# Cross-attention and decoder layer on one Trainium2 core: a new order of work in the first two groups of the first phase

## The chip, the cores and the metric

The kernel runs on one core of a Trainium2 chip. The metric is the device time of one launch in microseconds (us), the median of several runs. The core has TensorE (PE, matmuls), VectorE (DVE), ScalarE (ACT), GpSimd (POOL) and SyncE (SP), which issues most of the DMAs. Each engine runs its own program in order and waits on semaphores.

## The reference

Two layers over `x` (32 batches, 112 tokens, 512 wide). The first, which is all that this change touches, attends to a memory of 375 rows of 256:

```python
memory_proj = einsum('bme,de->bmd', memory, W_mem)
scores = einsum('bnd,bmd->bnm', x, memory_proj) / sqrt(512)
attn = softmax(scores)
memory_context = einsum('bnm,bmd->bnd', attn, memory_proj)
gate = sigmoid(einsum('bnf,df->bnd', concat([x, memory_context]), W_gate) + b_gate)
x = rmsnorm(x + gate * memory_context, norm_w)
```

The second is a decoder layer with two experts. `expert_mask` looks at the mask of the tokens (both a token and its successor padded), and each token goes through the one or the other set of weights (`v_*`, `l_*`): rotary self-attention, cross-attention to the memory, a gated MLP. Its order of tokens is by expert, so the kernel needs, before the first token is written, each token's rank among those of its expert.

## The kernel before, in words

Every fp32 operand is split into a high part (a copy rounded to the matmul's type, fp32r) and a low part (source minus high part), and each product is three matmuls: high by high (L111), high by low (L112), low by high (L113), in `split_products`. ScalarE makes most high parts, VectorE or GpSimd the low parts (`low`, L179). Weights come through a ring of 8 slots: SP loads (L188), ScalarE copies (`ring_high`, L201), GpSimd subtracts (`ring_low`, L179). Chunks 0 and 1 are for `u`, 2 and 3 for `context` (C_MC), 4 to 7 for `gate` (C_GATE).

The first phase takes the 32 batches in 8 groups of 4 (`NB`), and its order is written out by hand in one function for each engine: `a_sp`, `a_pool`, `a_act`, `a_pe`, `a_dve`. For a group g TensorE runs, in this order:

- `u(g)`: x times the combined weights, in two halves t of 128 rows; split by `u_high` (ACT L550) and `u_low` (DVE L752);
- `s0(g)`: the scores, u against the memory's transpose `m_hi`, `m_lo`, also in two halves t, with the four batches inside a half. The memory comes in two halves too: load (SP L471 or L485), `memory_high` (ACT L545), `memory_low` (DVE L179 with 1500 columns). The load of a half waits for the `memory_low` of the half before, since both use one buffer;
- softmax on DVE (L759, L763, L765) and ACT (L564);
- `gate(g-1)`: the gate of the group before, 72 matmuls; ACT applies tanh (L577), DVE forms the fused value in `gated` (L783, L786). The last of these releases the load of x for group g+1 (L474). Inside the fourth part are the transposes of the first two batches (L680, `transposed`);
- `attended(g, b)`: probabilities times memory (L688) for each batch, once DVE has copied the transposed probabilities (L797); then ACT copies the result (L589) and DVE subtracts (`attended_low`, L179 with 224 columns);
- `turn(g-1)`: transposes of the fused values (L698), squares on ACT (L603), power on POOL (L517), tokens on DVE (L823), and a scatter of the rows by POOL (L525);
- `context(g)`: 24 matmuls (L111 to L113).

Into group 0 and group 1 the one-time work is woven. `setup_pe_wc` multiplies W_mem and the memory's part of the gate weights (24 matmuls of 512 columns); `setup_dve_weights`, `setup_act_wc` and `setup_dve_wc` split its inputs and results. The ranks: `setup_dve` compares the mask (L330 to L332) and prepares the rotary positions (L334 to L339); `setup_pe` sums over the batches (L299, L300); `setup_dve_total` copies the totals (L343); `setup_pe_ranks` (L304, L306, L308) ranks them; `setup_dve_ranks` and `setup_dve_counts` (L348 to L381) count; `setup_pe_places` (L312) and `setup_dve_places` (L385 to L403) follow; `setup_dve_slots` (L410 to L433) makes the slots, and with them (L429) POOL starts six scatters of padding (L269 to L271), for which the squares of group 0 and `names(0)` (L814) wait.

## Time and profile before

| | |
|---|---|
| median of 3 runs | 2202.34 us (2202.33 to 2205.23) |
| the profiled execution's own time | 2200.88 us |
| its span | 2199.0 us |
| PE busy | 2103.6 us, 96% of the span |
| DVE, ACT, POOL busy | 1279.3, 1048.8, 879.2 us |
| granted TensorE clock, mean | 0.986 |
| first phase (groups 0 to 7) | about the first 340 us of the span |

A timeline row gives the start in us from the span's start, the duration in us (for a group, from its first start to its last end), the engine, the line, the operation, output and input, the count, and in brackets how long the engine had been idle and what released it. Matmuls overlap, so the distance between two starts, not the duration, is what one costs.

### The profile page before, as it was taken

What the parts mean: (1) busy time and instruction counts of PE and PEld (TensorE: products, weight loads), DVE (VectorE), ACT (ScalarE), POOL (GpSimd) and SP (SyncE); (2) the same over time, 40 slices, a digit from 0 to 9 for tenths busy, and PEclk for the clock granted to TensorE, in tenths of its full rate; (3) what the DMA queues carried; (4) which work ended last, traced back from release to release, by engine and by line L of the source; (5) the groups of instructions that cost most, each with busy time, mean ns of one, the idle gap of its engine ahead of it and who ended that gap; (6) DMA issues with size and microseconds to landing.
All of it is one profiled execution on the core that took longest, in us unless ns stands there. A gap on an engine that the chain in (4) does not pass through costs nothing.

```text
span 2199.0 us, 40731 instructions
## 1 busy us (share of the span) xinstructions
PE 2103.6 (96%) x16042; PEld 1821.3 (83%) x16042; DVE 1279.3 (58%) x2070; ACT 1048.8 (48%) x1875; POOL 879.2 (40%) x741
## 2 busy tenths in 40 slices
PE   7999999999888889997999999999999999999998
PEld 6899998888767777996899899877888888888888
DVE  6755547666589994445676676663444344443433
ACT  5344445343268774542665655654334333343334
POOL 2211026776635333633112112114455554555547
PEclk9999999999999999997999999999999999999999
DMA  6334344655564446656777777745343443434334
GB/s 241 123 131 147 115 158 151 238 204 212 200 202 141 138 136 239 242 199 197 229 231 228 218 216 222 213 138 194 115 138 119 134 151 114 139 117 125 119 94 130
DMA packets 155614, 373.70 MB, mean 170 GB/s; under 512 B 40160, under 2 KB 60992, under 8 KB 145696
## 3 DMA queue, kind: packets, MB, share of 16 engines
q1 hardware_dynamic: 136416, 310.70, 45.0%
q0 software_dynamic: 18720, 60.29, 7.5%
q8 instruction: 128, 2.10, 0.4%
q14 instruction: 62, 0.51, 0.1%
q10 hardware_dynamic: 288, 0.11, 0.0%
HBM read 269.28 MB, written 100.93 MB: 168 GB/s over the span
## 4 chain that ended last, share of the span: by engine, by line
PE 82%; DVE 9%; DMA 3%; ACT 3%; issue 2%; SPq 1%; POOLq 0%; POOL 0%; ACTq 0%; DVEq 0%
PE ps L111 21%; PE ps L113 21%; PE ps L112 21%; PE ps L1853 4%; PE ps L1885 3%; PE ps L1872 3%; DVE f_arena L1311 2%; DVE c_max L1306 2%; PE ps L688 2%; ACT f_arena L1767 1%; DMA f_arena<-qk_rows 1%; DVE c_sum L1317 1%; PE ps L1900 1%; PE ps L2201 1%; DVE f_arena L1328 1%
## 5 line engine op out<-in xcount | busy, mean ns | idle before, releaser
L111 PE MATMUL ps<-r_arena 128*128 128x512 f32 (+6 forms) x2410 | 893.1, 371 | 13.5 <-DVE r_arena L179 7.2
L113 PE MATMUL ps<-r_arena 128*128 128x512 f32 (+6 forms) x2410 | 882.5, 366 | 0.0
L112 PE MATMUL ps<-r_arena 128*128 128x512 f32 (+6 forms) x2410 | 882.2, 366 | 0.0
L179 POOL TENSOR_TENSOR r_arena<-f_arena,r_arena 128x512 fp32r<-128x512 f32 (+1 forms) x434 | 579.3, 1358 | 542.3 <-ACT r_arena L201 418.7
L111 PEld LDWEIGHTS ps<-r_arena 128*128 128x128 f32 (+2 forms) x2410 | 455.6, 189 | 77.1 <-POOL r_arena L179 6.2
L113 PEld LDWEIGHTS ps<-r_arena 128*128 128x128 f32 (+2 forms) x2410 | 454.5, 189 | 65.7
L112 PEld LDWEIGHTS ps<-r_arena 128*128 128x128 f32 (+2 forms) x2410 | 455.6, 189 | 60.3
L201 ACT CAST r_arena<-f_arena 128x512 fp32r<-128x512 f32 x400 | 236.3, 623 | 173.0 <-PE ps L113 133.3
L1979 DVE TENSOR_REDUCE e_negmax<-ps 112x2 f32<-112x750 f32 (+1 forms) x352 | 240.4, 720 | 95.4 <-PE ps L1853 94.2
L2289 DVE SCALAR_TENSOR_TENSOR f_arena<-f_arena,ps 128x512 f32<-128x512 f32 (+1 forms) x88 | 57.4, 652 | 235.1 <-ACT f_arena L2184 230.7
L1767 ACT ACTIVATE f_arena<-ps 125x896 f32<-125x896 f32 x192 | 166.4, 924 | 46.3 <-PE ps L1872 46.3
L2188 ACT CAST r_arena<-ps 128x512 fp32r<-128x512 f32 (+1 forms) x88 | 49.3, 561 | 243.4 <-DVE ps L2293 243.4
L179 DVE TENSOR_TENSOR r_arena<-ps,r_arena 128x512 fp32r<-128x512 f32 (+2 forms) x186 | 102.6, 562 | 89.5 <-ACT r_arena L2188 55.1
L1730 POOL DMA_INDIRECT cd_rows<-f_arena,slot_all x32 | 30.0, 937 | 289.4 <-ACT f_arena L1810 289.4
L1853 PE MATMUL ps<-r_arena 96*112 96x376 f32 x512 | 129.9, 354 | 10.7 <-DVE e_negmax L1979 4.5
L2293 DVE SCALAR_TENSOR_TENSOR ps<-f_arena,ps 128x512 f32<-128x512 f32 (+1 forms) x88 | 58.3, 663 | 107.1 <-PE ps L113 106.9
L2184 ACT ACTIVATE f_arena<-ps 128x512 f32<-128x512 f32 (+1 forms) x88 | 50.2, 571 | 138.2 <-PE ps L113 138.2
L1872 PE MATMUL ps<-r_arena 98*125 98x224 f32 x768 | 109.0, 278 | 2.6 <-DMA r_arena<-r_arena 0.3
L1872 PEld LDWEIGHTS ps<-r_arena 98*125 98x125 f32 x768 | 100.0, 190 | 12.3 <-ACT f_arena L1767 8.5
L1853 PEld LDWEIGHTS ps<-r_arena 96*112 96x112 f32 x512 | 82.3, 182 | 23.3 <-DVE e_negmax L1979 11.2
L517 POOL TENSOR_TENSOR a_rstd<-a_ss,minus_half 112x2 f32<-112x2 f32 x16 | 11.3, 705 | 202.5 <-DVE a_ss L807 202.4
L1171 POOL TENSOR_TENSOR f_arena<-f_arena 112x448 f32<-112x448 f32 x32 | 36.4, 1139 | 135.2 <-ACT f_arena L1211 135.2
(213 smaller groups left out, 2566.6 us busy)
## 6 DMA issues: line engine op xcount, KB each, us to landing
f_arena<-weights SPq DMA_DIRECT2D x400, 256.0 KB, 3.0
r_arena<-k_rows SPq DMA_DIRECT2D x192, 188.0 KB, 3.6
k_rows<-r_arena SPq DMA_DIRECT2D x64, 376.0 KB
f_arena<-rows SPq DMA_DIRECT2D x14, 1160.0 KB, 5.2
f_arena<-qk_rows SPq DMA_DIRECT2D x32, 448.0 KB
f_arena<-mem_n SPq DMA_DIRECT2D x8, 1536.0 KB, 6.9
f_arena<-mem_e SPq DMA_DIRECT2D x32, 376.0 KB, 4.9
f_arena<-mem_t SPq DMA_DIRECT2D x16, 750.0 KB, 6.0
```

Of the source, the lines that this page charges most:

```text
L111: first = pe.matmul(out, w_hi, x_hi, start=start, stop=False)
L112: pe.matmul(out, w_hi, x_lo, start=False, stop=False)
L113: return first, pe.matmul(out, w_lo, x_hi, start=False, stop=stop)
L179: return engine.tensor_tensor(out, source, high.bitcast(F32), ALU.subtract)
L201: act.copy(w_hi[:, m % RING, :], w_raw[:, m % RING, :]).then_inc(w_hi_made, 1)
L1767: act.activation(e_pt[:, u], ps[0:KC, at:at + 2, 0:4 * SEQ], ACT.Exp).then_inc(e_exp, 1)
L1853: last = pe.matmul(ps[0:SEQ, at + h - heads[0], 0:CEVEN], e_queries[b % 3][0:MAX_ROW, h % 2, h // 2, :], e_keys[b % 3][0:MAX_ROW, h // 2, ...
L1872: last = pe.matmul(ps[0:KC, 4 + 2 * (u % 2) + n // 2, n % 2 * 2 * SEQ:(n % 2 + 1) * 2 * SEQ], e_keys[b % 3][0:MAX_ROW + 2, pair, m], e_que ...
L1885: last = pe.matmul(ps[32 * a:32 * a + 32, 3, batch(n)], e_cv[b % 4][:, c, 4 * n + a, :], e_pt[:, NKC * t + c, half, batch(a)], start=c == ...
L1979: dve.tensor_reduce(e_negmax[:, b % 2, heads[0]:heads[-1] + 1], ps[0:SEQ, at:at + len(heads), 0:CTX], AX_X, ALU.max, negate=True).then_inc ...
L2289: dve.scalar_tensor_tensor(act_a[:, s, w], act_t[:, s, w], 1.0, ps[:, bank, w], ALU.add, ALU.mult).then_inc(f_acted, 1)
L2293: dve.scalar_tensor_tensor(ps[:, bank + 1, w], act_a[:, s, w], 0.5, ps[:, bank + 1, w], ALU.mult, ALU.mult).then_inc(f_glu_made, 1)
```

## The change

It moves instructions inside the first phase and changes one wait; no operation is added or taken out. `u_high`, `u_low` and the memory's splits of group 0 alternate by half; `s0` waits for each half of the memory by itself; the splits of the gate weights move ahead of group 0's attended copies on ACT; the mask part of `setup_dve` becomes `setup_dve_valid` ahead of the combined weights' splits on DVE, and the second of these splits moves behind two copies; `setup_pe` moves ahead of `context(0)` on PE; `setup_dve_total` moves ahead of the rest of `setup_dve`; `setup_dve_ranks` and `setup_dve_counts` move ahead of the first `u_low(1)`, and `memory_low(1, 1)` behind it; and for later groups the second `memory_low` moves out of the end of `gated` and behind the fourth copy of probabilities.

```diff
+        def setup_dve_valid(dve):
+            dve.wait_ge(const_loaded, 16 * len(loads))
+            dve.tensor_scalar(is_pad_s, mask_sb, 1, None, ALU.is_equal).then_inc(*d_steps.up())
+            dve.memset(ones_sb, 1.0).then_inc(*d_steps.up())
+            dve.wait_ge(*d_steps.now())
+            dve.tensor_tensor(is_v_s, is_pad_s[:, 0], is_pad_s[:, 1], ALU.mult).then_inc(s_isv, 1)
...
-            dve.wait_ge(const_loaded, 16 * len(loads))
-            now(dve.tensor_scalar(is_pad_s, mask_sb, 1, None, ALU.is_equal))
-            now(dve.memset(ones_sb, 1.0))
-            dve.tensor_tensor(is_v_s, is_pad_s[:, 0], is_pad_s[:, 1], ALU.mult).then_inc(s_isv, 1)
...
             for t in range(CT):
                 memory_high(0, t)
-            u_high(0)
+                u_high(0, t)
...
                     setup_act_wc(act)
-                    for m in range(C_MC, C_GATE):
+                    for m in range(C_MC, RING):
                         ring_high(act, m)
...
                     setup_act_consts(act)
-                    for m in range(C_GATE, RING):
-                        ring_high(act, m)
...
             def s0(g):
-                pe.wait_ge(a_m_lo, CT * (g + 1))
                 if g:
                     pe.wait_ge(a_mc_made, KT * g)
                 for t in range(CT):
+                    pe.wait_ge(a_m_lo, CT * g + t + 1)
                     pe.wait_ge(a_u_lo, CT * g + t + 1)
...
+                if g == 0:
+                    setup_pe(pe)
                 if g < GROUPS:
                     context(g)
-                if g == 0:
-                    setup_pe(pe)
...
-                if g + 2 < GROUPS:
-                    memory_low(g + 2, 1)
...
             for t in range(CT):
                 memory_low(0, t)
-            for t in range(CT):
                 u_low(0, t)
             setup_dve_weights(dve)
             softmax(0)
-            setup_dve_wc(dve)
+            setup_dve_valid(dve)
+            setup_dve_wc(dve, 0)
...
                     attended(0, 0)
                     attended(0, 1)
+                    setup_dve_wc(dve, 1)
                 if g < GROUPS:
                     for b in range(NB):
                         if b + 2 < NB:
                             attended(g, b + 2)
+                        if b == 1 and g and g + 1 < GROUPS:
+                            memory_low(g + 1, 1)
                         attended_low(g, b)
...
                 else:
+                    setup_dve_total(dve)
                     setup_dve(dve)
                     memory_low(1, 0)
                     x_low(1)
-                    setup_dve_total(dve)
-                    memory_low(1, 1)
+                    setup_dve_ranks(dve)
+                    setup_dve_counts(dve)
                 if g + 1 < GROUPS:
                     for t in range(CT):
                         u_low(g + 1, t)
                         if g == 0 and t == 0:
-                            setup_dve_ranks(dve)
-                            setup_dve_counts(dve)
+                            memory_low(1, 1)
```

How the order moves is seen at three places. The first is VectorE between group 0's attended copies and group 1's scores; before it reads (L343 is the copy of the totals, the 128x448 rows are x's low parts, the 128x1500 rows the memory's):

```order
L338 TENSOR_SCALAR f_arena<-f_arena 112x112
L339 TENSOR_TENSOR f_arena<-f_arena 112x112
L179 TENSOR_TENSOR r_arena<-f_arena,r_arena 128x1500
L179 TENSOR_TENSOR r_arena<-f_arena,r_arena 128x448 x4
L343 COPY f_arena<-ps 32x128
L179 TENSOR_TENSOR r_arena<-f_arena,r_arena 128x1500
L752 SCALAR_TENSOR_TENSOR r_arena<-ps,r_arena 128x448
```

and now (lines have shifted by a few numbers; L346 is the copy of the totals):

```order
L346 COPY f_arena<-ps 32x128
L337 CAST f_arena<-f_arena 112x112
L338 CAST f_arena<-f_arena 112x112
L339 TENSOR_SCALAR f_arena<-f_arena 112x112
L340 TENSOR_TENSOR f_arena<-f_arena 112x112
L341 TENSOR_SCALAR f_arena<-f_arena 112x112
L342 TENSOR_TENSOR f_arena<-f_arena 112x112
L179 TENSOR_TENSOR r_arena<-f_arena,r_arena 128x1500
L179 TENSOR_TENSOR r_arena<-f_arena,r_arena 128x448 x4
L351 COPY f_arena<-ps 112x32
```

The totals are copied before the six position steps and both sorts of low parts, and the ranks (L351) follow x's low parts at once.

The second place is ScalarE between the combined weights' splits and group 1's x. Before:

```order
L294 CAST r_arena<-ps 128x512 x2
L201 CAST r_arena<-f_arena 128x512 x2
L589 CAST r_arena<-ps 128x2x112 x4
L545 CAST r_arena<-f_arena 128x1500
L280 CAST causal<-f_arena 112x448
L281 CAST ident_b<-ident 128x128
L282 ACTIVATE half_b<-gate_b 128x4
L201 CAST r_arena<-f_arena 128x512 x4
L537 CAST r_arena<-f_arena 128x448 x4
```

and now:

```order
L294 CAST r_arena<-ps 128x512 x2
L201 CAST r_arena<-f_arena 128x512 x6
L589 CAST r_arena<-ps 128x2x112 x4
L547 CAST r_arena<-f_arena 128x1500
L280 CAST causal<-f_arena 112x448
L281 CAST ident_b<-ident 128x128
L282 ACTIVATE half_b<-gate_b 128x4
L539 CAST r_arena<-f_arena 128x448 x4
```

The four gate weights' copies (part of L201) now stand ahead of the four attended copies (L589).

The third is VectorE in group 1, as in groups 2 to 6: the end of `gated` and the attended copies. Before:

```order
L783 SCALAR_TENSOR_TENSOR f_arena<-f_arena 128x448
L786 SCALAR_TENSOR_TENSOR f_arena<-f_arena 128x448
L179 TENSOR_TENSOR r_arena<-f_arena,r_arena 128x1500
L797 COPY f_arena<-ps 125x336
L179 TENSOR_TENSOR r_arena<-ps,r_arena 128x2x112
L797 COPY f_arena<-ps 125x336
L179 TENSOR_TENSOR r_arena<-ps,r_arena 128x2x112 x3
```

and now:

```order
L782 SCALAR_TENSOR_TENSOR f_arena<-f_arena 128x448
L785 SCALAR_TENSOR_TENSOR f_arena<-f_arena 128x448
L794 COPY f_arena<-ps 125x336
L179 TENSOR_TENSOR r_arena<-ps,r_arena 128x2x112
L794 COPY f_arena<-ps 125x336
L179 TENSOR_TENSOR r_arena<-f_arena,r_arena 128x1500
L179 TENSOR_TENSOR r_arena<-ps,r_arena 128x2x112 x3
```

The 128x1500 row, the memory's low part, now follows both copies, with three of the four attended low parts behind it.

## Rows read from the trace of the kernel before

**Rows 1.** Waits of PE, 100 to 300 us: total us, times, longest us.

```profile
PE ps L688 <- DVE f_arena L797: 4.5, 5, 0.9
```

**Rows 2.** Timeline of PE, first 100 us: start, duration, and idle time before.

```profile
15.95 0.40 PE L111 MATMUL ps<-r_arena 128*112 128x376 f32 x1 [2.89 <-DVE r_arena L752]
...
21.67 0.40 PE L111 MATMUL ps<-r_arena 128*128 128x512 f32 x1
...
36.32 0.47 PE L111 MATMUL ps<-r_arena 128*128 128x448 f32 x1 [0.86 <-DVE r_arena L179]
...
46.71 0.58 PE L304 MATMUL ps<-f_arena 32*112 32x32 f32 x2 [4.61 <-DVE f_arena L343]
...
47.99 0.72 PE L111 MATMUL ps<-r_arena 128*128 128x448 f32 x1
...
55.60 0.39 PE L312 MATMUL ps<-f_arena 112*128 112x14 f32 x2 [1.06 <-DVE f_arena L381]
...
75.94 1.56 PE L688 MATMUL ps<-f_arena 125*128 125x112 f32 x12 [0.51 <-DVE f_arena L797]
...
81.48 4.56 PE L688 MATMUL ps<-f_arena 125*128 125x112 f32 x24 [1.98 <-DVE f_arena L797]
```

**Rows 3.** Busy time by stretch; the number after POOL is the granted clock.

```profile
18.00:20.00 2.00, 2.00 (x8) 1.94 (x8) 2.00 (x5) 1.00 (x2) 0.00 (x0) 0.50 0.99 350
...
36.30:41.40 5.10, 5.08 (x25) 4.46 (x25) 4.12 (x11) 5.07 (x11) 2.72 (x2) 1.00 0.11 14
...
46.70:55.80 9.10, 8.03 (x32) 7.06 (x32) 4.54 (x11) 1.09 (x2) 0.49 (x2) 0.76 0.30 106
...
79.30:86.00 6.70, 4.72 (x28) 4.54 (x28) 3.53 (x6) 0.79 (x3) 0.00 (x0) 0.75 0.52 176
```

**Rows 4.** Timeline of DVE, first 100 us.

```profile
16.95 3.63 DVE L179 TENSOR_TENSOR r_arena<-f_arena,r_arena 128x1024 fp32r<-128x1024 f32 x5 [0.61 <-ACT r_arena L287]
...
36.18 0.18 DVE L330 TENSOR_SCALAR f_arena<-f_arena 112x64 f32<-112x64 int32 x1
...
38.27 1.72 DVE L179 TENSOR_TENSOR r_arena<-f_arena,r_arena 128x1500 fp32r<-128x1500 f32 x1
40.67 5.78 DVE L179 TENSOR_TENSOR r_arena<-f_arena,r_arena 128x448 fp32r<-128x448 f32 x4 [0.68 <-ACT r_arena L537]
...
69.32 0.17 DVE L429 TENSOR_SCALAR f_arena<-f_arena 128x2 int32<-128x2 f32 x1
...
75.29 0.91 DVE L797 COPY f_arena<-ps 125x336 f32<-125x336 f32 x2
...
88.33 2.23 DVE L179 TENSOR_TENSOR r_arena<-f_arena,r_arena 128x448 fp32r<-128x448 f32 x4 [0.28 <-ACT r_arena L537]
...
91.02 2.72 DVE L823 SCALAR_TENSOR_TENSOR f_arena<-ps,a_rstd,norm 112x512 f32<-112x512 f32 x4
```

**Rows 5.** Timelines of ACT and of POOL, first 100 us.

```profile
86.58 0.60 ACT L603 ACTIVATE f_arena<-ps 112x512 f32<-112x512 f32 x1 [0.15 <-PE ps L698]
...
38.68 7.29 POOL L179 TENSOR_TENSOR r_arena<-f_arena,r_arena 128x512 fp32r<-128x512 f32 x4 [7.66 <-ACT r_arena L201]
```

**Rows 6.** Loads: first and last issue, time to landing (memory half; last two gate weights).

```profile
L471 SPq DMA_DIRECT2D f_arena<-mem_t x1: 439/439/439, 17.9 to 17.9; - x1
...
DMA to landing us min/median/max: 8.0/8.0/8.0
...
L188 SPq DMA_DIRECT2D f_arena<-weights x2: 450/468/485, 19.8 to 20.3; - x2
...
DMA to landing us min/median/max: 10.3/10.3/10.4
```

**Rows 7.** The chain that ended last: load and copy of memory (2, 1).

```profile
73.02 4.77 DMA f_arena<-mem_t
77.81 1.45 ACT r_arena L545
```

**Rows 8.** The last padding scatter, L271, issued at 77.1 us: time to landing.

```profile
DMA to landing us min/median/max: 7.1/7.1/7.1
```

More of the change, by code:

```diff
@@ L357, in setup_dve_weights, with setup_dve_wc @@
                 low(dve, wg_lo[:, k, :], wg_raw[:, k, :], wg_hi[:, k, :]).then_inc(s_lo, 1)
-        def setup_dve_wc(dve):
-            for t in range(CT):
-                dve.wait_ge(wc_hi_made, t + 1)
-                low(dve, wc_lo[:, t, :], ps[:, 6 + t, :], wc_hi[:, t, :]).then_inc(wc_lo_made, 1)
+        def setup_dve_wc(dve, t):
+            dve.wait_ge(wc_hi_made, t + 1)
+            low(dve, wc_lo[:, t, :], ps[:, 6 + t, :], wc_hi[:, t, :]).then_inc(wc_lo_made, 1)
         WHOLE = TILES - 1
@@ L545, in memory_high, with u_high @@
                 act.copy(m_hi[:, t, 0:NB * CTX], memt if g else memt_first[t]).then_inc(a_m_hi, 1)
-            def u_high(g):
-                for t in range(CT):
-                    act.wait_ge(a_u, CT * g + t + 1)
-                    act.activation(l_hi[:, t, :], ps[:, 6 + t, 0:NT], ACT.Copy,
-                                   scale=float(DIM) ** -0.5).then_inc(a_u_hi, 1)
+            def u_high(g, t):
+                act.wait_ge(a_u, CT * g + t + 1)
+                act.activation(l_hi[:, t, :], ps[:, 6 + t, 0:NT], ACT.Copy, scale=float(DIM) ** -0.5).then_inc(a_u_hi, 1)
             ring_high(act, 0)
@@ L617, in a_act @@
                 if g + 1 < GROUPS:
-                    u_high(g + 1)
+                    for t in range(CT):
+                        u_high(g + 1, t)
         def a_pe(pe):
@@ L832, in a_dve @@
                 memory_low(0, t)
-            for t in range(CT):
                 u_low(0, t)
```

## The prediction

> **What bounds the kernel now.** I read four views in this order. The page gives TensorE 2103.6 us of a span of 2199.0 (96%): it is the engine to save time on, in waits or in matmuls that run slowly. The waits of PE show where it idles in the first phase: from 100 to 300 us one wait alone, 0.9 us in each of five groups, for VectorE's copy L797 [rows 1]. The timeline of PE shows the others, all in the first 82 us: 2.89 us before the first scores, 0.86 before `context(0)`, 4.61 before the ranks (L304), 1.06 before L312, then 0.51 and 1.98 before L688 [rows 2]. The stretches show what a wait also costs: the granted clock was 0.50 (the lower level, 1.2 GHz) at 18 to 20 us, and averaged 0.76 at 46.7 to 55.8 and 0.75 at 79.3 to 86, each time after a wait of PE, and 1.00 at 36.3 to 41.4 [rows 3]. After the waits of 0.86 and 0.9 us the rows show no such loss. The timelines of the other engines say what is late in each place.
>
> The first phase hands a chain of work to the next without any fixed time in it, so what PE gains by the end of group 6 I carry to the end of the kernel.
>
> **Scores and weights of group 0.** The first scores wait for `u_low(0,0)`, which stood behind both memory halves. By halves, one memory low part (1.72 us [rows 4]) no longer stands in front: they start near 14.1 instead of 15.95 [rows 2], and end 1.9 us (clock as before) to 3.3 us earlier. Little of it arrives: the next matmuls (`setup_pe_wc`, at 21.67 [rows 2]) need the gate inputs' low parts, which VectorE finishes at 16.95 + 3.63 = 20.58 whatever the scores do [rows 4]. Gain 1.1 at most; a new wait of some 2 us stands in front, and if the clock falls there it takes up to 1.6 back (eight matmuls of 512 columns at half speed).
>
> **Group 0's attended part.** VectorE now makes one split less before its first copy, but ScalarE becomes the late one: four more copies stand ahead of its first L589, and the last of these needs a load issued at 20.3 that landed 10.4 us later, at 30.7 [rows 6]. With a copy of some 0.55 ScalarE is free at 31.25 and starts its first L589 there. From there: L589 0.35, low part 0.38, copy of the fourth batch 0.45 (two in 0.91 [rows 4]) to 32.4, its matmuls 1.4 (12 in 1.56, overlap included [rows 2]), L589 and low part 0.75: `context(0)` starts at 34.5 to 35.2 instead of 36.32 [rows 2]. I take 34.8, **1.5 us**. The two matmuls of `setup_pe` fall into the wait of 0.86 there. The mask work now stands in front of the first copy and waits for nine constant loads. No row shows their landing. The load behind them on the same queue, issued at 17.9, landed 8.0 later, at 25.9 [rows 6], and VectorE comes for them at about 25.2. So I take a wait of 0 to 0.7, hidden by ScalarE until 31.25. The farthest bound is their first use before, L330 at 36.2 [rows 4]: a rival.
>
> **From `context(0)` to group 1's scores.** 24 matmuls at 0.204 (25 in 5.1 us [rows 3]) end at 39.7. The wait of 4.61 goes: the totals are copied at 34.9. Then VectorE has six position steps (1.6 us of the 2.1 from L330 to the next memory half, 36.18 to 38.27 [rows 4]), `memory_low(1,0)` 1.7 and x's low parts. These took 5.78 us while GpSimd made the four gate weights' low parts (7.29 us); in group 1 the same four took 2.23 [rows 4, 5]. GpSimd now has its work at 30 to 35, beside copies and subtractions out of PSUM, and I take 2.23: x is ready at 40.4. The Trainium skill (GPSIMD Engine Reference, Specifications) says that GpSimd shares its SBUF interfaces with VectorE where a VectorE instruction has two SBUF inputs; the rows agree, and by that rule the gate weights' low parts would not be slowed where they now stand. The ranks' six matmuls took 1.28 (46.71 to 47.99 [rows 2]), less at the full clock: `u(1)` starts at 40.8, **5.7 more** (7.2 in all). Were x's low parts still 5.78 us, 3.5 of this chain would be lost.
>
> `u(1)` ran from 47.99 to 54.54 (55.60 less the wait of 1.06 [rows 2]), 6.55 us, in part at the lower clock; with PE busy right up to it I take 24 x 0.204 = 4.9: **1.6**. The wait of 1.06 before L312 goes too, since the counts are done at about 43.5: **1.06**. `s0(1)` starts at 46.0, 9.8 us early. Its second half needs `memory_low(1,1)`: load issued 38.2, landed 4 us later, ScalarE to 43.7, VectorE to 46.5, then `u_low(1,1)` 47.1; that half starts at 48.1. Covered with 1 us to spare.
>
> **Group 1.** VectorE is late here, not PE. Its places (L385) started as L312 ended, at 55.60 + 0.39 [rows 2]; now they start at 47.1, 8.9 early, and everything behind them (softmax, slots, `gated(0)`) is the same work: the copies for `attended(1)` come at 66.4 instead of 75.29, and PE, ready at 65.5, waits 1.5 instead of 0.51. 0.9 of the 9.8 is lost. Then the third copy no longer stands behind `memory_low(2,1)`, which stood behind a load of 4.77 us and a ScalarE copy of 1.45 [rows 7]. The wait of 1.98 [rows 2] with 0.2 of issue goes: **2.2**. The 24 matmuls behind it took 4.56 us where 12 such took 1.56, overlap included [rows 2]: at 1.4 for twelve, **1.8** if the clock holds. The load still stands ahead of ScalarE's L589: landed 68.9, copied 70.35, L589 70.7, fourth copy 71.55, needed 71.75. So it fits barely. `turn(0)` ends at 74.9, 12.9 early.
>
> What is late next is the padding. The last scatter, issued at 77.1, landed 7.1 later at 84.2 [rows 8], 14.7 us behind the slots (L429 ends at 69.49 [rows 4]). Now the slots come at 60.6, so it lands at 75.3, and the squares, which started at 86.58 behind PE's first turn [rows 5], could start at 73.55 and wait. `u(2)` needs the second token: 91.02 + 1.36 = 92.4, or 5.8 behind the first square. That gives 81.15 against an end of `context(1)` at 79.75: **-1.4**.
>
> **Groups 2 to 6.** The 0.9 us wait was for a copy behind `memory_low` (1.72). Now the copy goes first, as soon as PE's transposes are there. The low part then ends some 1 us before `turn` does, so `context` does not wait: 5 x 0.9 = **4.5** [rows 1]. Group 7 had no such low part.
>
> **Sum.** 1.5 + 5.7 + 1.6 + 1.06 - 0.9 + 2.2 + 1.8 - 1.4 + 4.5 = 16.0 us. The profiled execution's own time was 2200.88, so 2184.9 by it; the median of the runs is 1.46 higher, and I predict **2186.3**.
>
> The clock is the weakest term. The Trainium skill (TensorE: Matmul & The Clock Gate, What's actually happening) says that the watching runs free, so that one kernel shows different numbers of slow matmuls. By that rule the stretches of rows 3 could fall elsewhere in the new program, after its waits near 18.4, 65.5 and 79.8. From the rows each is worth up to 1.8 us.
>
> **Rivals.**
>
> (a) *A slow stretch returns in group 1* after the wait of 1.5 us, or `memory_low(2,1)` and the fourth copy miss by a little and PE stops again. Against: no loss after 0.9. For: a loss after 1.98. Gain 16.0 - 1.8 - 1.0 = 13.2: 2189.1. Chance 0.15.
>
> (b) *Groups 2 to 6 give nothing*: `memory_low` now stands ahead of three low parts that `context` needs. If it were slowed by more than the 1 us of slack, the wait moves from the copy to `context`. Gain 11.5: 2190.8. Chance 0.05.
>
> (c) *The change doesn't start where it says*: the constants land late, and VectorE holds the mask work in front of its first copy. PE's first attended matmuls then follow that landing. At the farthest bound, 36.2, the copy comes some 7.5 us later than I take and 8.5 are left: 2193.8. Chance 0.05.
>
> (d) *More*: slow stretches stay away at 18 us too and the scatters, with less beside them, land in time: + 0.5 + 1.4: 2184.4. Chance 0.13.
>
> (e) *Slower*: the clock falls at the wait before `u(2)` (79.8 to 81.2) and stays at the lower level. Matmuls then cost twice, so it outweighs the gain once 16 us of full-speed work have run so; a whole group (38 us) gives 2186.3 + 38 = 2224. Against: every stretch of the trace came back within 7 us, and groups 2 to 6 with waits of 0.9 never fell. Chance 0.02. The same page (Seeing it yourself) tells of records stuck at a low ratio for over 50 us; no row here shows that.
>
> **How the numbers follow.** Forecast 0.60. The range 2183.0 to 2190.6 takes in (d), the forecast with 2 us either way of clock and run, and (a); it leaves out (b), (c), (e). A measurement of this kernel can tell about 0.2% (4.4 us) from no change. Faster by more than that: all but (e) and worse mixtures of (b) and (c): 0.95; within it 0.03; slower 0.02.
>
> **What would show it.** L304 and L312 without a wait before them; `u(1)` near 41 us and 4.9 us long; `s0(1)` at 46; x's low parts in about 2.2 us; the wait before L304 replaced by none longer than 2.3 us anywhere; the attended matmuls of group 1 in one clock; ScalarE's squares of group 0 waiting for the last scatter; no wait for the copy from 100 to 300 us, and none for L179 or L589 in its place. A first L589 after 33 us, x's low parts over 4 us, or a granted clock of 0.5 after 55 us would make me wrong.

## The result and the profile after

| | before | changed |
|---|---|---|
| median, runs taken side by side | 2202.34 us (5 runs, 2198.42 to 2205.23) | 2190.04 us (5 runs, 2186.0 to 2190.69) |
| the profiled execution's own time | 2200.88 us | 2186.00 us |
| its span | 2199.0 us | 2184.1 us |
| PE busy | 2103.6 us | 2096.5 us |

The ratio is 0.9937, with an interval of 0.9925 to 0.9948: 13.9 us less, and between 11.5 and 16.5 us by the interval. The prediction said faster, 2186.3 us, within 2183.0 to 2190.6. The direction is right and the range holds the median, near its upper end. The working is best judged inside the trace, where each term has a place.

The timeline of PE of the changed kernel, rows at the places of [rows 2], and the last row at the end of the first phase:

```profile
14.05 0.33 PE L111 MATMUL ps<-r_arena 128*112 128x376 f32 x1
...
20.55 0.47 PE L111 MATMUL ps<-r_arena 128*128 128x512 f32 x1 [2.20 <-DVE r_arena L179]
...
34.74 0.47 PE L111 MATMUL ps<-r_arena 128*128 128x448 f32 x1 [0.21 <-DVE r_arena L179]
...
39.80 0.38 PE L304 MATMUL ps<-f_arena 32*112 32x32 f32 x2
...
40.53 0.45 PE L111 MATMUL ps<-r_arena 128*128 128x448 f32 x1
...
45.84 0.40 PE L111 MATMUL ps<-r_arena 128*112 128x376 f32 x1
...
67.75 1.56 PE L687 MATMUL ps<-f_arena 125*128 125x112 f32 x12 [2.21 <-DVE f_arena L794]
...
71.14 2.84 PE L687 MATMUL ps<-f_arena 125*128 125x112 f32 x24
...
73.82 1.91 PE L697 MATMUL ps<-ident,f_arena 128*112 128x128 f32 x16
...
82.38 0.47 PE L111 MATMUL ps<-r_arena 128*128 128x448 f32 x1 [1.78 <-DVE f_arena L820]
...
319.41 1.91 PE L1013 MATMUL ps<-ident,f_arena 128*128 128x128 f32 x16
```

The ranks (L304) have no wait in front, `u(1)` starts at 40.53, `s0(1)` at 45.84. The 24 matmuls of the third and fourth batch take 2.84 us, where [rows 2] had 4.56. Three waits of about 2 us are left: before the product of the weights (20.55), before `attended(1)` (67.75) and before `u(2)` (82.38). In the profile of before the last row stood at 335.79, so the first phase ends 16.4 us sooner.

The waits of PE of the changed kernel, 0 to 100 us, in the columns of [rows 1]; from 100 to 300 us this view has no row any more, where [rows 1] had 4.5 us in five waits:

```profile
PE ps L111 <- DVE r_arena L179: 8.4, 3, 6.0
PE ps L687 <- DVE f_arena L794: 2.6, 2, 2.2
PE ps L111 <- DVE f_arena L820: 1.8, 1, 1.8
```

The timeline of VectorE of the changed kernel, with the answers to [rows 4]:

```profile
24.90 0.19 DVE L326 TENSOR_SCALAR f_arena<-f_arena 112x64 f32<-112x64 int32 x1
...
34.60 0.27 DVE L346 COPY f_arena<-ps 32x128 f32<-32x128 f32 x1
34.80 1.19 DVE L337 CAST f_arena<-f_arena 112x112 f32<-112x112 int32 x1
...
37.30 3.86 DVE L179 TENSOR_TENSOR r_arena<-f_arena,r_arena 128x1500 fp32r<-128x1500 f32 x5
...
47.77 0.22 DVE L387 TENSOR_SCALAR f_arena<-f_arena 128x7 f32<-128x7 f32 x1
...
61.13 0.17 DVE L431 TENSOR_SCALAR f_arena<-f_arena 128x2 int32<-128x2 f32 x1
...
67.10 0.92 DVE L794 COPY f_arena<-ps 125x336 f32<-125x336 f32 x2
...
76.47 0.29 DVE L811 COPY f_arena<-cos_sin 112x256 f32<-112x256 f32 x1 [1.68 <-DMA cd_rows<-f_arena,pad_slot]
```

The mask work (L326) runs at 24.90 without a wait, so the constants were there. The memory's low part and x's four together take 3.86 us, against 1.72 and 5.78 in [rows 4]. The row of L337 is the one I had not foreseen: an int32 to fp32 cast of 112x112 takes 1.19 us. The same cast took 0.21 us before.

The timeline of GpSimd of the changed kernel, at that cast:

```profile
27.49 7.42 POOL L179 TENSOR_TENSOR r_arena<-f_arena,r_arena 128x512 fp32r<-128x512 f32 x6 [17.14 <-ACT r_arena L201]
34.85 1.07 POOL L263 MEMSET f_arena<- 128x1160 f32 x1
```

The memset ends at 35.92 and the cast at 35.99. ScalarE of the changed kernel has the other two places, its first attended copy and the first square of group 0:

```profile
31.06 0.58 ACT L589 CAST r_arena<-ps 128x224 fp32r<-128x224 f32 x2
...
76.47 0.60 ACT L601 ACTIVATE f_arena<-ps 112x512 f32<-112x512 f32 x1 [2.10 <-DMA cd_rows<-f_arena,pad_slot]
```

### The profile page after: what moved, and what is told of

Same layout as the page of the kernel before. It is cut to its first block, busy times and chain, and to the rows that moved or that the text cites. A ratio compares the mean times of both kernels' runs of the same rounds, so it can differ in the third digit from the quotient of the medians.

```text
span 2184.1 us, 40739 instructions
## 1 busy us (share of the span) xinstructions
PE 2096.5 (96%) x16042; PEld 1815.5 (83%) x16042; DVE 1276.0 (58%) x2070; ACT 1049.1 (48%) x1875; POOL 876.5 (40%) x741
## 4 chain that ended last, share of the span: by engine, by line
PE 80%; DVE 8%; DMA 5%; ACT 3%; SPq 2%; issue 2%; POOL 0%; POOLq 0%; ACTq 0%; DVEq 0%
PE ps L111 20%; PE ps L113 20%; PE ps L112 20%; PE ps L1853 4%; PE ps L1885 3%; PE ps L1872 3%; DMA f_arena<-qk_rows 2%; DVE f_arena L1311 2%; DVE c_max L1306 2%; PE ps L687 2%; ACT f_arena L1767 1%; DMA f_arena<-weights 1%; PE ps L1230 1%; PE ps L1900 1%; PE ps L2201 1%
## 5 line engine op out<-in xcount | busy, mean ns | idle before, releaser
L111 PE MATMUL ps<-r_arena 128*128 128x512 f32 (+6 forms) x2410 | 890.3, 369 | 13.9 <-DVE r_arena L179 8.6
L201 ACT CAST r_arena<-f_arena 128x512 fp32r<-128x512 f32 x400 | 236.5, 623 | 175.4 <-PE ps L113 129.6
```

Of the source, the lines that this page charges most:

```text
L111: first = pe.matmul(out, w_hi, x_hi, start=start, stop=False)
L201: act.copy(w_hi[:, m % RING, :], w_raw[:, m % RING, :]).then_inc(w_hi_made, 1)
```

## The experiments

Each variant starts from the changed kernel, except where it says from the kernel before. Medians are compared with the kernel before on the same chip: 2200.94 us for the first four, 2204.43 for the next four, 2201.35 for the last two. Beside the median stands the landmark that proved sharper: the first row of L1013, the end of the first phase, 335.79 before and 319.41 after. Each of these times comes from one profiled execution. A variant counts by its number here: variant 3 is the kernel of experiment 3.

**1. The memory's low part moved, and nothing else** (from the kernel before).

```diff
-                if g + 2 < GROUPS:
-                    memory_low(g + 2, 1)
...
+                        if b == 1 and g and g + 1 < GROUPS:
+                            memory_low(g + 1, 1)
                         attended_low(g, b)
```

> The kernel before with one part of the change alone: the second memory low part of groups 2 to 7 behind the copies. My theory: the waits before L688 in groups 2 to 6 go, each worth 1.16 us from start to start (the idle column shows 0.9 because a matmul's modelled end overlaps), so 5.8 us; in group 1 the wait of 1.98 and the slow stretch behind it go too, but then the squares wait for the last padding scatter, which leaves 2 to 2.5 there. Sum about 8 us faster, near 2194. Rival (the low part becomes late for context): a wait of PE for L179 before context in groups 2 to 6, and under 3 us gained.

Measured: 2193.76 us, ratio 0.9963 (0.9949 to 0.9976); the phase ends at 326.76, 9.0 us sooner. Of the 9.0 us, 2.8 are there when `u(2)` starts (89.75 instead of 92.50) and 6.3 come in groups 2 to 6. No wait is left from 100 to 300 us, and the third batch of group 1 starts without one and at the full clock:

```profile
79.16 2.84 PE L688 MATMUL ps<-f_arena 125*128 125x112 f32 x24
...
326.76 1.91 PE L1013 MATMUL ps<-ident,f_arena 128*128 128x128 f32 x16
```

**2. The same move taken back, and all else kept.**

```diff
+                if g + 2 < GROUPS:
+                    memory_low(g + 2, 1)
...
-                        if b == 1 and g and g + 1 < GROUPS:
-                            memory_low(g + 1, 1)
                         attended_low(g, b)
```

> The changed kernel with that same part undone. If the parts add up, it loses 5.8 us in groups 2 to 6 against the changed kernel and up to 2 us in group 1, where the wait for the load of the memory's second half comes back: 6 to 8 us slower than the changed kernel, so about 7 us faster than before, near 2196. If the gain of the set-up parts were given back later, it would stand within 3 us of before.

Measured: 2197.05 us, ratio 0.9976 (0.9966 to 0.9986). Its timeline and waits of PE:

```profile
74.89 4.56 PE L687 MATMUL ps<-f_arena 125*128 125x112 f32 x24 [1.80 <-DVE f_arena L796]
...
329.29 1.91 PE L1013 MATMUL ps<-ident,f_arena 128*128 128x128 f32 x16
```

```profile
PE ps L687 <- DVE f_arena L796: 4.5, 5, 0.9
```

The five waits of 0.9 are back, and so is the wait in group 1 (1.80) with its 24 slow matmuls: 4.56 us, the very number of [rows 2]. The first two groups' new order is worth 6.5 us by itself, the low part's move 9.0. They add up to 15.5, against 15.8 for the repeat of the changed kernel below, which has the same slow product of the weights as variant 2. At the landmark the two parts add up within 0.3 us.

**3. GpSimd's two memsets at the start of its program**, away from VectorE's position steps.

```diff
+            pool.memset(tok[:, 0:PADS, :], 0.0).then_inc(pads_zeroed, 1)
+            pool.wait_ge(pads_zeroed, 1)
+            pool.memset(tok[:, PADS:NB, DIM:ROW], 0.0).then_inc(pads_zeroed, 1)
             for m in range(RING):
                 ring_low(pool, m)
-            pool.memset(tok[:, 0:PADS, :], 0.0).then_inc(pads_zeroed, 1)
-            pool.wait_ge(pads_zeroed, 1)
-            pool.memset(tok[:, PADS:NB, DIM:ROW], 0.0).then_inc(pads_zeroed, 1)
```

> The changed kernel with GpSimd's two memsets for the padding moved to the program's start, where it idles. Theory: the integer cast L337, 1.19 us in the changed kernel beside the memset and 0.21 before, is slowed by that memset; it goes back to about 0.2, VectorE's places, slots and first copies of group 1 come 1.0 us sooner, and PE's wait before the first attended matmuls of group 1 falls from 2.2 to about 1.2. About 1 us faster than the changed kernel. Rival (the cast is slow for another reason, such as ScalarE's copies beside it): the cast stays at 1.2 and nothing moves.

Measured: 2187.4 us, ratio 0.9934 (0.992 to 0.9947); the phase ends at 319.38. VectorE and GpSimd of this variant:

```profile
35.88 0.57 DVE L337 CAST f_arena<-f_arena 112x112 f32<-112x112 int32 x1
```

```profile
28.93 7.45 POOL L179 TENSOR_TENSOR r_arena<-f_arena,r_arena 128x512 fp32r<-128x512 f32 x6 [18.83 <-ACT r_arena L201]
```

The cast is shorter, not yet 0.2. GpSimd's last low part ends at 28.93 + 7.45 = 36.38, the cast at 36.45. What holds the cast is thus whatever GpSimd has running, not the memset as such. The 1 us that was expected is not there at the landmark: the phase ends 0.03 us sooner than in the first profile of the changed kernel and 0.6 sooner than in its repeat. PE still waits 2.00 us before `attended(1)`, and this profile has a slow stretch there.

**4. Group 0's squares written elsewhere** (with edit 3). Only their sum is used; as their own output they now take the buffer of the probabilities, in bf16, instead of the token rows, so that ScalarE need not wait for the padding scatters.

```diff
+        p0_half = fv(12252, (NB * CTX,), SEQ).bitcast(BF16)
...
-                    else:
-                        act.wait_ge(pads_scattered, 16 * 3 * PADS)
+                    aside = g == 1
...
-                        act.activation(tok[0:SEQ, b, 0:DIM], ps[0:SEQ, turn_bank(b), :], ACT.Square,
+                        act.activation(p0_half[:, b * DIM:b * DIM + DIM] if aside else tok[0:SEQ, b, 0:DIM], ps[0:SEQ, turn_bank(b), :], ACT.Square,
```

> The kernel of the run memset_early, and the squares of group 0 write their unused result (in bf16) to the probabilities' buffer, so they need not wait for the padding scatters; only the names on VectorE still do. Theory: the wait of 2.10 us of ScalarE for the last scatter and the wait of 1.78 of PE before u(2) go or shrink to under 0.5: 1.5 to 2 us faster than memset_early, some 2.5 to 3 faster than the changed kernel. Rival: VectorE's names wait for the scatter as long, with x's low parts behind them, and PE's wait stays above 1.2.

Measured: 2184.81 us, ratio 0.9918 (0.9903 to 0.9932), the lowest ratio of all, though the first phase shows only a small part of that gain; the phase ends at 318.93, 0.45 before variant 3. ScalarE of this variant:

```profile
74.98 0.60 ACT L601 ACTIVATE f_arena<-ps 112x512 bf16<-112x512 f32 x1
...
77.39 1.97 ACT L540 CAST r_arena<-f_arena 128x448 fp32r<-128x448 f32 x4 [1.14 <-DMA f_arena<-x_t]
```

The squares no longer wait, but two of them later ScalarE waits 1.14 us for group 2's x, and PE still 1.02 before `u(2)` (1.78 in the changed kernel's first profile, 1.06 in its repeat, both with the scatters). So the scatters do hold the squares of the changed kernel, and right behind them stands the load of x: x's high parts start at 77.39, against 77.63 in that first profile. The 1.5 to 2 us that were expected over variant 3 are not there for that reason.

**5. The wait before the product of the weights filled** with ten matmuls whose result nobody reads. This and variant 9 add work that is no part of the computation.

```diff
             s0(0)
+            for _ in range(10):
+                pe.matmul(ps[:, 4, 0:NT], x_parts[0][0][:, 0, 0:P], x_parts[0][0][:, 0, :], start=True, stop=True)
             setup_pe_wc(pe)
```

> The changed kernel with ten matmuls of 448 columns, whose result nobody reads, in the wait of 2.2 us between the first scores and the weights' product. In the changed kernel's profile the granted clock stayed at 1.00 there; in three profiles of its variants it read 0.76 from 20 to 27 us and the product's 24 matmuls took 7.15 us instead of 5.56. Theory: the fall comes from the wait and varies from run to run; filled, the clock reads 1.00 from 13 to 27 us in any run, the product ends by 26.3, context(0) starts by 34.9, and the median falls by 0.5 to 1.5 us against the changed kernel (2190.0). Rival (the fall has nothing to do with the wait): 0.76 again.

Measured: 2187.98 us, ratio 0.9924 (0.9905 to 0.9943); the phase ends at 319.80. The product ran at the full clock and `context(0)` started at 35.10. `context(0)` is thus 0.36 us later than in the first profile, which had the full clock there too, and 0.8 sooner than in the repeat. In this profile the clock fell one wait later, before `attended(1)`, as it did in variants 3, 7 and 8, which have no unread matmuls. This variant's timeline of PE:

```profile
20.89 0.47 PE L111 MATMUL ps<-r_arena 128*128 128x512 f32 x1 [0.20 <-DVE r_arena L179]
...
68.10 2.20 PE L687 MATMUL ps<-f_arena 125*128 125x112 f32 x12 [2.19 <-DVE f_arena L796]
...
73.12 2.84 PE L687 MATMUL ps<-f_arena 125*128 125x112 f32 x24
```

Twelve matmuls took 2.20 us behind a wait of 2.19; in the changed kernel they took 1.56 behind one of 2.21. From these twelve to the start of `turn(0)` it is 7.70 us here and 6.07 there, so the same wait can cost 1.6 us more or nothing. Little of it reaches the end: `u(2)` starts at 82.81 instead of 82.38, as the wait for the padding shrinks from 1.78 to 0.23.

**6. The copy of the totals back behind x's low parts.**

```diff
-                    setup_dve_total(dve)
                     setup_dve(dve)
                     memory_low(1, 0)
                     x_low(1)
+                    setup_dve_total(dve)
```

> The changed kernel with the copy of the totals back behind the position steps, the memory half and x's low parts. Theory: the wait of 4.61 before was mostly x's low parts slowed by GpSimd's gate splits; with those already done, x's low parts still end near 41.2, the copy at 41.4, and PE waits 1.7 us before L304: group 1 starts 1.5 to 2 us later, 1 to 2 us slower in all. Rival (the place of the copy itself made the wait): 4 us or more before L304 and 4 us slower.

Measured: 2188.36 us, ratio 0.9936 (0.9918 to 0.9953); the phase ends at 323.64. VectorE, GpSimd and PE of this variant:

```profile
35.89 1.75 DVE L337 CAST f_arena<-f_arena 112x112 f32<-112x112 int32 x1
```

```profile
36.49 1.08 POOL L263 MEMSET f_arena<- 128x1160 f32 x1
```

```profile
43.05 0.38 PE L304 MATMUL ps<-f_arena 32*112 32x32 f32 x2 [1.89 <-DVE f_arena L346]
```

The wait before L304 comes back, 1.89 us of it. Against the repeat, which has the same slow product, the places, which lead to the slots, start at 50.12 instead of 49.28, the last scatter lands 1.8 us later (7.4 us after its issue instead of 6.4), and `u(2)` starts at 85.04 instead of 83.16. At the landmark the difference is 3.7 us, and only 1.9 of it is there when `u(2)` starts. The rest comes inside group 2, mostly from the clock, which fell behind PE's wait of 2.11 us before `u(2)`. The stretch from 85 to 90 us of this variant (the number after POOL is the granted clock, 1.00 in the repeat):

```profile
85.00:90.00 5.00, 4.96 (x17) 4.47 (x18) 1.90 (x3) 0.69 (x2) 3.41 (x4) 0.66 0.54 167
```

So the later copy itself costs between 0.8 us, its delay of the slots, and 1.9; the other 1.8 need not come in each execution. The median does not show either: it is lower than that of the changed kernel.

**7. The copies of the gate weights back behind the constants** on ScalarE.

```diff
-                    for m in range(C_MC, RING):
+                    for m in range(C_MC, C_GATE):
                         ring_high(act, m)
...
                     setup_act_consts(act)
+                    for m in range(C_GATE, RING):
+                        ring_high(act, m)
```

> The changed kernel with ScalarE's four gate weight copies back behind the constants. Theory: ScalarE's first L589 no longer waits for the last load (31.06 us) and context(0) starts 0.5 to 1 us sooner, but the copies then delay x's high parts by 2.2 us and GpSimd's four low parts run beside x's low parts, which take over 5 us instead of 2.2: PE waits inside or before u(1), and the copies for group 1's attended part come 2.5 to 4 us later. 2.5 to 4 us slower than the changed kernel. Rival (no contention, the slowness of x's low parts before was ScalarE's): x's low parts in under 3 us and within 1 us of the changed kernel.

Measured: 2190.68 us, ratio 0.9941 (0.9924 to 0.9959); the phase ends at 322.66, 2.7 us behind the repeat. VectorE and GpSimd of this variant:

```profile
35.77 0.20 DVE L337 CAST f_arena<-f_arena 112x112 f32<-112x112 int32 x1
...
40.06 5.49 DVE L179 TENSOR_TENSOR r_arena<-f_arena,r_arena 128x448 fp32r<-128x448 f32 x4 [1.08 <-ACT r_arena L539]
```

```profile
28.82 2.51 POOL L179 TENSOR_TENSOR r_arena<-f_arena,r_arena 128x512 fp32r<-128x512 f32 x2 [19.01 <-ACT r_arena L201]
38.08 6.99 POOL L179 TENSOR_TENSOR r_arena<-f_arena,r_arena 128x512 fp32r<-128x512 f32 x4 [6.75 <-ACT r_arena L201]
```

With GpSimd's subtractions beside them x's low parts take 5.49 us again, as in [rows 4], and two waits of 0.75 appear in `u(1)`. So this move pays by keeping two engines' two-input subtractions apart, as the prediction had it. And the cast, with GpSimd idle from 31.33 to 38.08, takes 0.20 us.

**8. The halves undone**: group 0's scores wait for both memory halves, as before. On ScalarE both copies of `u(0)` go behind both memory halves again, too.

```diff
                 memory_low(0, t)
+            for t in range(CT):
                 u_low(0, t)
...
+                if g == 0:
+                    pe.wait_ge(a_m_lo, CT)
                 for t in range(CT):
-                    pe.wait_ge(a_m_lo, CT * g + t + 1)
+                    if g:
+                        pe.wait_ge(a_m_lo, CT * g + t + 1)
```

> The changed kernel with group 0's scores waiting for both halves of the memory, as before. Theory: the first scores start near 15.9 instead of 14.05 and end near 20.5 to 21.7; the weights' product starts then instead of at 20.55, so at most 1.1 us go in front, and ScalarE's wait for the gate weights (free at 31.1) hides half of it: 0 to 1 us slower, which these runs can hardly tell. The wait of 2.9 us puts the slow stretch into the scores instead of the product. Rival (the earlier scores carry through to the end): 1.9 us or more slower.

Measured: 2186.57 us, ratio 0.9925 (0.9908 to 0.9943); the phase ends at 318.92. Timeline of PE of this variant:

```profile
15.90 0.40 PE L111 MATMUL ps<-r_arena 128*112 128x376 f32 x1 [2.34 <-DVE r_arena L755]
...
20.67 0.47 PE L111 MATMUL ps<-r_arena 128*128 128x512 f32 x1 [0.42 <-DVE r_arena L179]
...
35.19 0.47 PE L111 MATMUL ps<-r_arena 128*128 128x448 f32 x1 [0.21 <-DVE r_arena L179]
```

The scores start 1.85 us later, the product only 0.12 and `context(0)` 0.45, and at the landmark nothing is lost. The halves only move the wait from the scores to behind them, and no gain of theirs is seen at the end. The slow stretch that was expected in the scores, behind the wait of 2.34, did not come either: the granted clock is 1.00 from 15 to 20 us.

**9. Edits 3, 4 and 5 together, and nine matmuls in the wait before `attended(1)`.**

```diff
                     pe.wait_ge(a_mn_loaded, 16 * (g + 1))
+                    for _ in range(9 if g == 1 else 0):
+                        pe.matmul(ps[:, 0, 0:NT], x_parts[1][0][:, 0, 0:P], x_parts[1][0][:, 0, :], start=True, stop=True)
```

> The changed kernel with four more edits: the memsets at the start, the squares aside, ten unread matmuls in the wait before the weights' product, and nine in the wait before group 1's attended part. Theory: the two waits are where the clock falls in some runs and not in others, so with both filled the granted clock reads 1.00 from 6 to 95 us; GpSimd is done with the gate splits by 35, so the cast L337 takes 0.2; the first u_low(2) comes by 84.3 instead of 85.7. Phase one ends 1.5 to 2.5 us sooner than in the changed kernel's profile; the median lies 2 to 4 us under that of the changed kernel in the same rounds. Rival: the clock falls anyway, the unread matmuls only delay, and it stands within 1 us of the changed kernel.

Its result stands with that of the next.

**10. The changed kernel again**, unedited, on the same chip.

> The changed kernel itself once more, beside the run combined on one chip. Theory: its own runs again spread over some 4 to 6 us, and its profile may show a slow stretch of TensorE at 20 to 27 us or at 60 to 75 us that the first profile did not; where it does, phase one ends 1 to 2 us later than there. Rival: the same profile as the first, within 0.3 us in phase one.

Measured: 2190.31 us, ratio 0.9944 (0.9931 to 0.9958), for the combination; 2189.71 us, ratio 0.9942 (0.9929 to 0.9956), for the repeat. The phase ends at 317.62 and at 319.95. The combination has the granted clock at 1.00 throughout the first 95 us, and its cast takes 0.20 us, with no work of GpSimd beside it after 34.56. So the first phase ends 2.3 us sooner than in the repeat and 1.8 sooner than in the first profile, and nothing of it is seen in the median, which was expected 2 to 4 us lower.

The repeat shows the slow product again. Its stretch from 20 to 27 us, then that of the changed kernel's first profile (the number after POOL is the granted clock):

```profile
20.00:27.00 7.00, 6.34 (x22) 5.14 (x23) 5.59 (x17) 3.14 (x9) 0.00 (x0) 0.76 1.04 351
```

```profile
20.00:27.00 7.00, 6.37 (x30) 5.24 (x30) 5.77 (x18) 3.71 (x11) 0.00 (x0) 1.00 1.03 358
```

One program, one wait (2.18 and 2.20 us), and 0.76 or 1.00. `context(0)` starts at 35.93 in the repeat instead of 34.74, yet the phase ends only 0.5 us later: the last scatter was issued 1.5 us later but landed after 6.4 us instead of 7.5, and so `u(2)` starts only 0.8 later.

**Why medians don't separate these variants.** Behind the first phase all kernels do the same work. From the first row of L1013 to the end of the span it took 1863.2 us before, 1864.7 after, 1862.4 in the repeat, 1863.7 in the combination and 1870.7 in variant 5. The stretch from 340 to 2180 us, of the repeat and then of variant 5:

```profile
340.00:2180.00 1840.00, 1772.90 (x14161) 1515.09 (x14159) 1069.16 (x1629) 892.38 (x1532) 806.15 (x663) 0.99 0.55 174
```

```profile
340.00:2180.00 1840.00, 1775.76 (x14139) 1516.84 (x14138) 1067.69 (x1624) 891.36 (x1530) 804.06 (x661) 0.98 0.55 174
```

Variant 5 keeps PE busy 2.9 us longer in that stretch, with 22 matmuls fewer recorded and at a lower mean clock. A part that no edit touches thus varies by 8 us, more than edits 3 to 9 are worth. The matmuls of a group vary a little too, at a granted clock of 1.00: from the start of `context` to the transposes inside the next gate it is between 25.53 and 25.76 us, with one such block for each of groups 2 to 6. The five take 127.7 us in the repeat and 128.7 in the combination, which was 3.2 us ahead when `u(2)` started and 2.3 at the end. I judge edits 3 to 9 by the landmark and by their own rows alone.

## Why the prediction was right, and where not

The table follows the sum term by term. The measured column takes differences of start times in the two profiles, before minus after.

| step | predicted | measured |
|---|---|---|
| to `context(0)` | 1.5 | 1.6 |
| to `u(1)`: the wait of 4.61 | 5.7 | 5.9 |
| to `s0(1)`: full clock, and the wait at L312 | 1.6 + 1.06 | 2.5 |
| VectorE late in group 1 | -0.9 | -1.8 |
| to `turn(0)`: the wait of 1.98 and the slow stretch | 2.2 + 1.8 | 3.9 |
| to `u(2)`: padding | -1.4 | -1.9 |
| groups 2 to 6 | 4.5 | 6.3 |
| end of the first phase | 16.0 | 16.4 |

The sum lies closer to the trace than its terms do. Groups 2 to 6 gave 1.8 us more than forecast; the late VectorE and the padding took 1.4 more. That these nearly cancel is luck, and so is the full clock behind the waits of 2.20 and 2.21 us in this one profile.

**What held.** The late engine behind `context(0)` was ScalarE, first L589 at 31.06 (31.25 predicted). That holds for this profile; in the repeat the slow product made PE late, and L589 first ran at 31.46. The ranks' wait went, and nothing longer than 2.21 us took its place. x's low parts took 2.2 us once GpSimd's subtractions were moved; variant 7 shows that this is the reason. The clock held through `u(1)`, and the slow stretch of group 1 went with the wait that variant 2 brings back. The load and copy of memory (2, 1) fit with nothing to spare and no wait. The padding is what comes next, as variant 4 shows. A small slip: `setup_pe` has four matmuls and not two (L299 and L300, two each), which took 0.7 us from start to start before.

**Groups 2 to 6, the largest miss.** I priced the wait at the 0.9 us of idle time in [rows 1]. The rows of PE around it, before and then after, show more:

```profile
118.69 1.50 PE L688 MATMUL ps<-f_arena 125*128 125x112 f32 x12
...
121.42 2.93 PE L688 MATMUL ps<-f_arena 125*128 125x112 f32 x24 [0.90 <-DVE f_arena L797]
```

```profile
108.57 1.50 PE L687 MATMUL ps<-f_arena 125*128 125x112 f32 x12
...
110.24 2.84 PE L687 MATMUL ps<-f_arena 125*128 125x112 f32 x24
```

From start to start it is 2.73 us before and 1.67 after: 1.06, since the modelled end of the last matmul overlaps the next start where there is no wait. The 24 matmuls behind the wait are another 0.1 longer. Five times 1.16 is 5.8. The other 0.5 is not the wait: it lies in the blocks of matmuls from `context` to the next transposes, which take 25.53 to 25.75 us each at a granted clock of 1.00. The five took 128.4 us before and 127.9 after. Variant 1, without the waits, has blocks of both lengths, so this part need not be the edit's.

**VectorE in group 1.** I had the places 8.9 us early, and they are 8.2: L337 took 1.0 us longer than before, held until GpSimd's memset ended. In the combination, with `context(0)` at the same time (34.77 against 34.74) and a cast of 0.20, the places start at 46.88 instead of 47.77: 0.9 of it comes back. The prediction had moved GpSimd's low parts to 30 to 35 us and never asked what stands behind them on GpSimd. Its own rule, that every queue a moved step passes counts, names the omission.

**Padding.** The last scatter landed at 76.4, 15.1 us behind the slots, where I carried over 14.7 from [rows 4, 8]; and the slots came at 61.3 rather than 60.6.

**Scores by halves.** The prediction gave them at most 1.1 us and put no term for them into the sum. Variant 8 shows that nothing arrives. It also warned of the new wait and its slow product. The first profile happened to escape it; the repeat and five of the variants (2, 3, 4, 6, 7) did not, and in these `context(0)` starts 1.0 to 1.3 us later than in the first profile.

**The rivals.** (b) fell: no wait of `context` came in groups 2 to 6. (c) fell: the mask work ran at 24.90. (a), a slow stretch in group 1, occurred in neither profile of the changed kernel, but variants 3, 5, 7 and 8, whose matmuls there are the same, show a mean clock of 0.89 at 60 to 75 us, so it does occur in some executions. (d) was half right: the stretch at 18 us was fast, the scatters were not in time. (e) was not seen in the changed kernel. In variant 6 the clock did fall behind the wait before `u(2)`, and came back: from 90 to 100 us it reads 1.00.

**From 16.4 to 13.9.** The profiled execution was 14.9 us shorter: 16.4 in the first phase, less the 1.5 that the untouched rest took longer. The median differs by 12.3 us and the ratio says 13.9, both inside what the rest varies by itself. The forecast put the median 1.46 us above the profiled execution, as before; this time the profiled execution was the fastest of the five, and the median lies 4.0 above it. Of the 3.7 us by which the median exceeds the forecast, 2.6 are this, and 1.1 are in the profiled execution itself. Whether a small part of the gain is systematically given back there stays open: 8 us of variation would hide it.

## What to carry to other kernels

Price a removed wait of TensorE from the start of one matmul to the start of the next, in the trace with and without it, not by the idle column; and count the slow matmuls behind it as a term that may or may not come. When a step moves to another engine's idle time, list what follows it on the same queue and what that will now run beside. When a change is worth less than the rest of the program varies, look at a landmark directly behind the edited part, and at a repeat of the unedited kernel.

## What the runs showed of the hardware that I had not expected

**A cast inside SBUF is held by GpSimd, not slowed.** L337, int32 to fp32, 112x112, takes 0.20 to 0.21 us with GpSimd idle (variants 7 and 9, and the kernel before). Else it ended 0.06 or 0.07 us after the GpSimd instruction that was running: 1.19 us long (memset until 35.92, cast until 35.99), 0.57 (low part until 36.38, cast until 36.45), 1.75 (memset until 37.57, cast until 37.64). Where another GpSimd instruction started while it was held, it waited for that too: in the changed kernel it began at 34.80, before the last low part ended at 34.91, and then outlasted the memset. A copy out of PSUM was not held: L346 took its 0.27 us at 34.60, with GpSimd's subtraction running until 34.91.

The subtractions with two SBUF inputs are not merely slowed either; VectorE's and GpSimd's take turns. The last of each in variant 7:

```profile
43.85 1.71 DVE L179 TENSOR_TENSOR r_arena<-f_arena,r_arena 128x448 fp32r<-128x448 f32 x1
```

```profile
43.40 1.68 POOL L179 TENSOR_TENSOR r_arena<-f_arena,r_arena 128x512 fp32r<-128x512 f32 x1
```

GpSimd's ends at 45.08 and VectorE's at 45.56, 0.48 us later; alone such a one takes 0.56. GpSimd's in turn ends 1.14 us behind VectorE's one before, which ended at 43.94; alone it takes 1.24. So x's four took 5.5 to 5.8 us instead of 2.2. The Trainium skill (Advanced Engine Details and Errata, VectorE Performance Modes) says that the second port of VectorE is shared with GpSimd, and that GpSimd's instructions and VectorE's two-port ones "interfere/block eachother". For the cast these rows agree, and here it is a block for the whole of GpSimd's instruction. Which mode the cast ran in, no row shows.

**The clock after a wait of about 2 us differs between executions of the same work.** Behind waits of 2.16 to 2.38 us before the product the granted clock of 20 to 27 us was 0.76 in six profiles and 1.00 in one, and one of the six was of the same program as the one. The 24 matmuls then took 7.0 to 7.2 us instead of 5.6. With that wait filled (variants 5 and 9) it was 1.00 both times: this fits a fall caused by the wait, but two profiles do not prove it. Before `attended(1)`, the clock fell behind waits of 1.68, 2.00, 2.18 and 2.19 us and not behind 1.54, 1.80, 2.19, 2.20 and 2.21, so the length of the wait alone does not tell.
